# A graph network on one core: query projection and its nonlinearity computed in the first gather instead of the second

## The chip, the core and the metric

The kernel runs on one core of a Trainium2 chip. The metric is device time in microseconds (us) of one execution. The core has a matrix engine (TensorE, PE in the profile), VectorE (DVE), ScalarE (ACT), GpSimd (POOL), SyncE (SP), which here only issues DMAs, and 16 DMA engines that all queues share. Each engine runs its own instructions in order and waits on semaphores for the others.

## The reference

One layer over 12500 nodes of width 256 and 212500 edges, all in float32. With xn = layernorm(x):

```
gnn:  agg = segment_sum((xn @ W)[src] * weight, dst) + b ; elu, twice (the second reads the first's output)
mix:  Q = elu(xn @ Wq) + 1 ; K = elu(xn @ Wk) + 1 ; v = (xn @ Wv) / L
      KV = sum over nodes of K^T v, per head ; Z = 1 / (Q . sum K + 1e-6)
      msg = layernorm(((Q @ KV) * Z * L) @ Wm) * g1 + b1
      h = relu(concat(xn, msg) @ W1) @ W2 ; mix = xn + layernorm(h) * g2 + b2
x = x + gnn + mix ; x = x + mixture_of_experts(layernorm(x))
```

Q is needed against KV, and KV is a sum over all nodes. Q itself depends on xn and Wq alone.

## The kernel before, in words

`program` runs five stages in turn: `prepare` (layernorm of x, tables, constants), `gather` for layer 1, `gather` for layer 2, `route` and `experts`.

A gather has 104 turns (`loops` of two, u = 0, 1, buffers by u). In each, GpSimd issues 16 indirect DMAs (line 460), each of which fetches 128 rows of 256 floats by the indices in `idx`; the rows are double-buffered by turn. GpSimd may start a turn when TensorE has begun the turn before, which releases the other half of `rows` (`rows_used`). TensorE multiplies the rows with one-hot selections (`sel`, line 411) in four groups of 32 matmuls (`window_products`, line 403), the first two groups when the first eight DMAs have landed, the others when all have. VectorE adds the four sums into `agg` at places that it loads from a table into registers (lines 494 to 500), and releases the next turn with `turn_added`.

Beside that, each gather carries dense work on tiles of 128 nodes, one tile a turn for the first 98 turns, cut into places between the groups: `mix.pe(pe, i, u, place)` is called ahead of the first group (place 0), behind the first, second and third (1, 2, 3) and behind the fourth (4), and `mix.dve` and `mix.act` have places of their own. The order on each engine is that of the calls.

In the first gather the mixer is `keys_values`: TensorE turns the tile (line 784), ScalarE copies it out as `xt`, TensorE projects keys and values (line 790) and adds their product to `kv_total` (796). `dense_first` follows eight turns behind: the layer's product `z`, its elu and the store of h.

In the second gather the mixer is `attend`. For tile t, `queries` times `m.kv` (961), VectorE's `message` (1037 to 1042), transposes (968), the product with w_m (974), layernorm, transposes (979), the hidden product (987, of `xt` and the normed message), relu, the output product (947), a second layernorm one turn later and the store of `mix` (926). For tile t + 1, in the same turn, it makes the queries: the tile is turned (933) behind the transposes of the message; ScalarE copies `xt` (1079); the product with w_q (940) stands behind the transposes of the normed message; VectorE takes min(q, 0) (1020) behind its adds and after the release of TensorE; ScalarE takes exp (1083) ahead of its relu; VectorE adds max(q, 0) (1055) at the head of the next turn. `dense_second` follows eight turns behind with the second layer's product, residual, layernorm and gate.

SyncE's turn issues the next idx (430) once the rows of two turns ago have landed, the next tile (917), the store of `mix` and waits for its landing (926 to 928), and then the dense stores and loads (1269 to 1277).

Of the kernel before, what the change touches and what calls it, by code (L numbers as in the profile page):

```python
# [12 lines left out]
P = 128  # L13
# [104 lines left out]
def prepare(nc, m):  # L118

    with ExitStack() as ctx:  # L120
        def sb(name, shape, dt):
# [54 lines left out]
            (m.w_q[:, :, :], m.in_w_q.rearrange("(k p) n -> p k n", p=P)),  # L176
# [173 lines left out]
def gather(nc, m, layer, source, mixer, denser):  # L350
# [4 lines left out]
    with ExitStack() as ctx:  # L355
# [63 lines left out]
        with nc.Block(f"gather{layer}") as block:  # L419
            @block.sync  # L420
            def _(sp):
                for u in range(2):
                    sp.dma_start(idx[:, u, :], m.in_src[u]).then_inc(idx_loaded[u], 16)
                    mix.load(sp, u, u)
                mix.load_weights(sp)
                dense.load_weights(sp)

                def turn(i, u):
                    sp.wait_ge(rows_loaded[u][BANKS - 1], 16 * GROUP * SUB * i)
                    sp.dma_start(idx[:, u, :], m.in_src[bass.ds(2 * i + u, 1)].rearrange("o p c -> (o p) c")  # L430
                                 ).then_inc(idx_loaded[u], 16)
# [300 lines left out]
def keys_values(nc, m, sb, sem, ps, shared):  # L732
# [3 lines left out]
    w_v = sb("w_v", [P, KD, D])  # L736
    tile = sb("kv_tile", [P, 2, D])
    xt = sb("kv_xt", [P, KD, P])
# [6 lines left out]
    total = ps("kv_total", KD, KVS)  # L745

    weights_loaded = sem("kv_weights_loaded")
# [16 lines left out]
    def load_weights(sp):  # L764
        for to, of in ((w_k, m.in_w_k), (w_v, m.in_w_v)):
            sp.dma_start(to[:, :, :], of.rearrange("(k p) n -> p k n", p=P)).then_inc(weights_loaded, 16)
# [4 lines left out]
    def pe_begin(pe):  # L771
        pe.wait_ge(weights_loaded, 32)

        nc.tensor.matmul(total[:, :, :], m.ident[:, :], m.zeros[:, :].rearrange("p (k n) -> p k n", k=KD),
                         start=True, stop=False)

    def pe(pe, i, u, place):
        t = 2 * i + u
        if not has_tile(i, u):
            return  # L780
        if place == 0:
            pe.wait_ge(tile_loaded[u], 16 * i + 16)
            for h in range(KD):
                last = nc.tensor.transpose(turned[:, h, :], tile[:, u, h * P:(h + 1) * P], m.ident[:, :])
            last.then_inc(tile_turned, 1)
        if place == 1:
            pe.wait_ge(xt_ready, t + 1)
            for n, w in enumerate((w_k, w_v)):
                for k in range(KD):
                    last = nc.tensor.matmul(proj[n][:, 0, :], xt[:, k, :], w[:, k, :], start=(k == 0), stop=(k == KD - 1))  # L790
# [23 lines left out]

    def act(act, i, u, place):
        t = 2 * i + u
        if place or not has_tile(i, u):
            return
        act.wait_ge(tile_turned, t + 1)
        nc.scalar.copy(xt[:, :, :], turned[:, :, :]).then_inc(xt_ready, 1)  # L820
# [6 lines left out]
        nc.scalar.activation(k_exp[:, :], k_min[:, :], ACT.Exp).then_inc(k_exp_ready, 1)  # L827

# [15 lines left out]
    mix.dve, mix.act, mix.after = dve, act, after  # L844
    mix.store = lambda sp, i, u: None
# [5 lines left out]
def attend(nc, m, sb, sem, ps, shared):  # L851
# [6 lines left out]
    q_min = sb("q_min", [P, KD, P])  # L858
    queries = q_min
# [17 lines left out]
    tile_ps = ps("tile_ps", KD, P)  # L877
    query_ps = tile_ps
# [7 lines left out]
    tile_turned = sem("tile_turned")  # L886
    xt_ready = sem("xt_ready")
    query_projected = sem("query_projected")
    q_min_ready = sem("q_min_ready")
    q_exp_ready = sem("q_exp_ready")  # L890
    queries_ready = sem("queries_ready")
# [38 lines left out]
    def turn_tile(pe, t, u, i):  # L930
        pe.wait_ge(tile_loaded[u], 16 * i + 16)
        for h in range(KD):
            last = nc.tensor.transpose(tile_ps[:, h, :], tile[:, u, h * P:(h + 1) * P], m.ident[:, :])
        last.then_inc(tile_turned, 1)

    def project_queries(pe, t, u):
        pe.wait_ge(xt_ready, t + 1)
        for h in range(KD):
            for k in range(KD):
                last = nc.tensor.matmul(query_ps[:, h, :], m.w_q[:, k, h * P:(h + 1) * P], xt[:, u, k, :],  # L940
                                        start=(k == 0), stop=(k == KD - 1))
        last.then_inc(query_projected, 1)

# [7 lines left out]
    def pe_begin(pe):  # L951
        turn_tile(pe, 0, 0, 0)
        project_queries(pe, 0, 0)

    def pe(pe, i, u, place):
        t = 2 * i + u
        if place == 1:
            if has_tile(i, u):
                pe.wait_ge(queries_ready, t + 1)
                for h in range(KD):  # L960
                    last = nc.tensor.matmul(num_ps[:, h, :], queries[:, h, :], m.kv[:, h, :], start=True, stop=True)
# [3 lines left out]
        if place == 2 and has_tile(i, u):  # L965
# [4 lines left out]
            if has_tile(i, u, 1):  # L970
                turn_tile(pe, t + 1, 1 - u, i + u)
# [4 lines left out]
        if place == 4 and has_tile(i, u):  # L976
# [4 lines left out]
            if has_tile(i, u, 1):  # L981
                project_queries(pe, t + 1, 1 - u)
# [35 lines left out]
    def min_query(dve, t):  # L1018
        dve.wait_ge(query_projected, t + 1)
        nc.vector.tensor_scalar(q_min[:, :, :], query_ps[:, :, :], 0.0, None, ALU.min).then_inc(q_min_ready, 1)  # L1020

# [25 lines left out]
    def dve_begin(dve):  # L1047
        min_query(dve, 0)

    def dve(dve, i, u, place):  # L1050
        t = 2 * i + u
        if place == 0 and has_tile(i, u):
            dve.wait_ge(q_exp_ready, t + 1)

            nc.vector.scalar_tensor_tensor(queries[:, :, :], query_ps[:, :, :], 0.0, q_min[:, :, :],
                                           ALU.max, ALU.add).then_inc(queries_ready, 1)
# [5 lines left out]
        if place == 2:  # L1062
            if not before_first(i, u, 1) and has_tile(i, u, -1):
                output(dve, t - 1, 1 - u)
            if has_tile(i, u):
# [11 lines left out]
    def copy_tile(act, t, u):  # L1077
        act.wait_ge(tile_turned, t + 1)
        nc.scalar.copy(xt[:, u, :, :], tile_ps[:, :, :]).then_inc(xt_ready, 1)

    def exp_query(act, t):
        act.wait_ge(q_min_ready, t + 1)
        nc.scalar.activation(q_min[:, :, :], q_min[:, :, :], ACT.Exp).then_inc(q_exp_ready, 1)

    def act_begin(act):
# [3 lines left out]
        copy_tile(act, 0, 0)  # L1089
        exp_query(act, 0)  # L1090

    def act(act, i, u, place):
        t = 2 * i + u
        if place == 0:
# [5 lines left out]
            if has_tile(i, u, 1):  # L1100
                copy_tile(act, t + 1, 1 - u)
        if place == 1 and has_tile(i, u):
            guess_sd(act, t, 0)
        if place == 2 and has_tile(i, u):
# [5 lines left out]
            if has_tile(i, u, 1):  # L1110
                exp_query(act, t + 1)
# [3 lines left out]
    mix.load, mix.free, mix.store = load, free, store  # L1115
    mix.pe_begin, mix.pe, mix.dve_begin, mix.dve, mix.act_begin, mix.act = pe_begin, pe, dve_begin, dve, act_begin, act
    mix.pe_end = mix.dve_end = mix.act_end = lambda engine: None
# [785 lines left out]
def program(nc, ins, out, scratch):  # L1903
# [8 lines left out]
    m.mix = scratch("mix", [NP, D], F32)  # L1912
    m.x2 = scratch("x2", [UNITS * P, D], F32)
# [4 lines left out]
    with ExitStack() as ctx:  # L1918
# [20 lines left out]
        m.w_q = sb("w_q", [P, KD, D])  # L1939
# [72 lines left out]
```

## Time and profile before

| | us |
|---|---|
| median of 3 runs | 5139.43 |
| lowest, highest | 5133.67, 5143.25 |
| profiled execution | 5136.3 |
| its span | 5134.5 |
| mean granted clock of TensorE | 0.847 of full |
| busy: PE, DVE, ACT, POOL | 4113.3, 2643.0, 846.1, 3474.6 |
| moved by DMA | 639.48 MB, mean 125 GB/s |

The span runs from the first to the last instruction, 1.8 us less than the execution's time. Busy times overlap, so they don't add up to the span. The first gather lies at about 150 to 2265 us, the second at 2275 to 4441, routing and experts behind it. `[2.42 <-DMA rows<-h,idx]` behind an instruction means that its engine had idled 2.42 us before it and that this DMA ended the wait. A granted clock of 1 is 2.4 GHz, 0.5 is 1.2 GHz.

### The profile page before, as it was taken

What the parts mean: (1) busy time and instruction counts of PE and PEld (TensorE: products, weight loads), DVE (VectorE), ACT (ScalarE), POOL (GpSimd) and SP (SyncE); (2) the same over time, 40 slices, a digit from 0 to 9 for tenths busy, and PEclk for the clock granted to TensorE, in tenths of its full rate; (3) what the DMA queues carried; (4) which work ended last, traced back from release to release, by engine and by line L of the source; (5) the groups of instructions that cost most, each with busy time, mean ns of one, the idle gap of its engine ahead of it and who ended that gap; (6) DMA issues with size and microseconds to landing.
All of it is one profiled execution on the core that took longest, in us unless ns stands there. A gap on an engine that the chain in (4) does not pass through costs nothing. (4 is left out here: it accounts for less than half of the span.)

```text
span 5134.5 us, 87736 instructions
## 1 busy us (share of the span) xinstructions
PE 4113.3 (80%) x24996; PEld 3765.1 (73%) x24997; DVE 2643.0 (51%) x9389; ACT 846.1 (16%) x2617; POOL 3474.6 (68%) x3768
## 2 busy tenths in 40 slices
PE   0477777777777777759989898899888998689998
PEld 0476776767766667658888888888888887568887
DVE  7433333333333333345676666666666765554444
ACT  2001000010000000001222222222222221241111
POOL 0577777777777777757777777777777777235554
PEclk9867777777777777658999999999999998599999
DMA  7444444444444444434455545555555455322222
GB/s 212 134 116 119 117 118 118 119 118 118 118 119 118 118 118 119 115 84 118 138 148 148 152 145 146 145 153 146 146 150 150 144 146 152 99 68 76 73 73 69
DMA packets 361208, 639.48 MB, mean 125 GB/s; under 512 B 105581, under 2 KB 230381, under 8 KB 360989
## 3 DMA queue, kind: packets, MB, share of 16 engines
q0 software_dynamic: 171840, 469.16, 32.2%
q1 hardware_dynamic: 181621, 155.12, 9.9%
q10 hardware_dynamic: 7632, 13.77, 0.7%
q8 instruction: 61, 1.00, 0.1%
q14 instruction: 54, 0.44, 0.0%
HBM read 548.73 MB, written 89.00 MB: 124 GB/s over the span
## 5 line engine op out<-in xcount | busy, mean ns | idle before, releaser
L403 PEld LDWEIGHTS sums<-sel,rows 128*128 128x128 f32 x13312 | 1939.0, 227 | 782.7 <-DMA rows<-xn,idx 414.2
L403 PE MATMUL sums<-sel,rows 128*128 128x64 f32 x13312 | 1944.8, 310 | 688.9 <-DMA rows<-xn,idx 312.1
L460 POOL DMA_INDIRECT rows<-xn,idx x1664 | 1577.9, 948 | 644.8 <-issue 634.1
L460 POOL DMA_INDIRECT rows<-h,idx x1664 | 1585.7, 953 | 578.8 <-issue 527.1
L411 DVE TENSOR_SCALAR sel<-cols,rel_now,wgt_now 128x64 f32<-128x64 f32 x3360 | 781.8, 338 | 7.8
L417 DVE TENSOR_TENSOR agg<-agg,sums 128x128 f32 x832 | 240.6, 289 | 786.0 <-issue 570.0
L612 DVE TENSOR_TENSOR pre<-z,b_g 128x256 f32<-128x256 f32 x98 | 41.6, 425 | 558.2 <-PE z L607 558.2
L1816 PE MATMUL e_hidden_ps<-tokens_t,w 128*128 128x256 f32 x1248 | 277.9, 381 | 0.9 <-ACT tokens_t L1840 0.9
L1828 PE MATMUL y_ps<-w,e_hidden 128*128 128x256 f32 x1248 | 277.0, 380 | 0.0
L987 PE MATMUL hidden_ps<-xt,w 128*128 128x128 f32 x1568 | 250.1, 282 | 21.2 <-ACT msg_t L1108 21.0
L1816 PEld LDWEIGHTS e_hidden_ps<-tokens_t,w 128*128 128x128 f32 x1248 | 238.5, 191 | 34.1 <-ACT tokens_t L1840 1.3
L1828 PEld LDWEIGHTS y_ps<-w,e_hidden 128*128 128x128 f32 x1248 | 235.0, 191 | 30.5
L987 PE MATMUL hidden_ps<-msg_t,w 128*128 128x128 f32 x1568 | 239.4, 275 | 0.0
L987 PEld LDWEIGHTS hidden_ps<-xt,w 128*128 128x128 f32 x1568 | 208.3, 193 | 38.6 <-ACT msg_t L1108 38.6
L947 PE MATMUL row_ps<-w,hidden 128*128 128x256 f32 x784 | 215.9, 426 | 0.0
L987 PEld LDWEIGHTS hidden_ps<-msg_t,w 128*128 128x128 f32 x1568 | 207.1, 192 | 0.0
L790 PE MATMUL kv_proj<-w_k,kv_xt 128*128 128x256 f32 x392 | 198.0, 661 | 0.0
L808 DVE TENSOR_SCALAR k_min<-kv_proj 128x256 f32<-128x256 f32 x98 | 41.6, 425 | 282.1 <-PE kv_proj L790 282.1
L947 PEld LDWEIGHTS row_ps<-w,hidden 128*128 128x128 f32 x784 | 164.8, 221 | 23.3
L974 PE MATMUL row_ps<-w_m,msg_t 128*128 128x256 f32 x392 | 114.4, 416 | 65.0 <-ACT msg_t L1099 65.0
L790 PE MATMUL kv_proj<-w_v,kv_xt 128*128 128x256 f32 x392 | 164.7, 567 | 0.0
L1014 ACT ACTIVATE ln_var<-var 128x1 f32<-128x1 f32 x196 | 39.7, 203 | 729.1 <-DVE var L996 729.1
(227 smaller groups left out, 4701.9 us busy)
## 6 DMA issues: line engine op xcount, KB each, us to landing
rows<-xn,idx POOLq DMA_INDIRECT x1664
rows<-h,idx POOLq DMA_INDIRECT x1664
w<-in_ffn_w SPq DMA_DIRECT2D x16, 1024.0 KB, 7.8
ln_rows<-in_x SPq DMA_DIRECT2D x52, 256.0 KB
xn<-ln_normed ACTq DMA_DIRECT2D x52, 256.0 KB, 4.4
kv_tile<-xn SPq DMA_DIRECT2D x98, 128.0 KB, 2.2
h<-h_rows SPq DMA_DIRECT2D x98, 128.0 KB, 2.1
tile<-xn SPq DMA_DIRECT2D x98, 128.0 KB
```

The costliest lines, as they stand in the source:

```text
L403: last = nc.tensor.matmul(sums[:, g, h, :], rows[:, u, k, h * P:(h + 1) * P], sel[:, u, k, :], start=(c == 0), stop=(c == GROUP - 1))
L411: last = nc.vector.tensor_scalar(sel[:, u, k, :], m.cols[:, :], rel_now[:, u, k:k + 1], wgt_now[:, u, k:k + 1], ALU.is_equal, ALU.mult)
L417: return nc.vector.tensor_tensor(window, window, sums[:, g, :, :], ALU.add)
L460: nc.gpsimd.indirect_dma_start(out=rows[:, u, k, :], out_offset=None, in_=source, in_offset=bass.IndirectOffsetOnAxis(ap=idx[:, u, k:k + 1 ...
L612: nc.vector.tensor_tensor(pre[:, :], z, b_g1[:, :], ALU.add).then_inc(pre_ready, 1)
L790: last = nc.tensor.matmul(proj[n][:, 0, :], xt[:, k, :], w[:, k, :], start=(k == 0), stop=(k == KD - 1))
L808: nc.vector.tensor_scalar(k_min[:, :], proj[0][:, 0, :], 0.0, None, ALU.min).then_inc(k_min_ready, 1)
L947: last = nc.tensor.matmul(row_ps[1], hidden[:, o, :], m.w_2[:, o, :], start=(o == 0), stop=(o == F1 // P - 1))
L974: last = nc.tensor.matmul(row_ps[0], msg_t[:, k, :], m.w_m[:, k, :], start=(k == 0), stop=(k == KD - 1))
L987: last = nc.tensor.matmul(hidden_ps[:, o, :], m.w_1[:, k, o * P:(o + 1) * P], of, start=(k == 0), stop=(k == 2 * KD - 1))
L1816: last = nc.tensor.matmul(hidden_ps[f % HB], m.w1[u][:, k, f * P:(f + 1) * P], tokens_t[:, k, :], start=(k == 0), stop=(k == KD - 1))
L1828: last = nc.tensor.matmul(y_ps[tt], hidden[:, f, tt * P:(tt + 1) * P], m.w2[u][:, f, :], start=(f == 0), stop=(f == FC - 1))
```

## The change

The first gather computes the queries and stores them, and it stores the transposed rows `xt` as well; the second loads both. w_q is loaded with w_k and w_v and no longer among the constants of `prepare`. In `keys_values` `xt` gets two buffers and there are new buffers for `q_min` and `queries` and a bank for the product. SyncE calls `mix.load_more` behind `mix.store`, and `mix.stored` at the end.

In `gather`:

```diff
                     mix.load(sp, u, u)
+                    mix.load_more(sp, 0, u)
...
                     if has_tile(i - 1, u):
                         mix.store(sp, i - 1, u)
+                    if has_tile(i, u):
+                        mix.load_more(sp, i, u)
                     dense.sp(sp, i - 1, u)
...
+                mix.stored(sp)
                 dense.sp_end(sp)
```

In `keys_values`, the first gather (`exp_query` is called behind `exponential` of the dense part, as ScalarE's place 2):

```diff
+        if place == 2:          # TensorE
+            if not before_first(i, u, 1):
+                wait_apart(pe, queries_ready, t, m.pe_passed)
+            for h in range(KD):
+                for k in range(KD):
+                    last = nc.tensor.matmul(query_ps[:, h, :], w_q[:, k, h * P:(h + 1) * P], xt[:, u, k, :],
+                                            start=(k == 0), stop=(k == KD - 1))
+            last.then_inc(query_projected, 1)
...
                                            ALU.max, ALU.add).then_inc(keys_ready, 1)   # VectorE, place 2
+            dve.wait_ge(query_projected, t + 1)
+            nc.vector.tensor_scalar(q_min[:, :, :], query_ps[:, :, :], 0.0, None, ALU.min).then_inc(q_min_ready, 1)
+        if place == 3:
+            if not before_first(i, u, 2):
+                wait_apart(dve, q_stored[u], 32 * i, m.passed)
+            dve.wait_ge(q_exp_ready, t + 1)
+            nc.vector.scalar_tensor_tensor(queries[:, u, :, :], query_ps[:, :, :], 0.0, q_min[:, :, :],
+                                           ALU.max, ALU.add).then_inc(queries_ready, 1)
...
+        if not before_first(i, u, 2):     # ScalarE, ahead of the copy of xt
+            wait_apart(act, q_stored[u], 32 * i, m.act_passed)
...
+    def exp_query(act, i, u, place):
+        if place == 2 and has_tile(i, u):
+            act.wait_ge(q_min_ready, 2 * i + (u + 1))
+            nc.scalar.activation(q_min[:, :, :], q_min[:, :, :], ACT.Exp).then_inc(q_exp_ready, 1)
...
+    def store(sp, i, u):
+        t = 2 * i + u
+        sp.wait_ge(xt_ready, t + 1)
+        sp.dma_start(m.xt[bass.ds(t * P, P), :], xt[:, u, :, :].rearrange("p k n -> p (k n)")).then_inc(q_stored[u], 16)
+        sp.wait_ge(queries_ready, t + 1)
+        sp.dma_start(m.qt[bass.ds(t * P, P), :], queries[:, u, :, :].rearrange("p k n -> p (k n)")
+                     ).then_inc(q_stored[u], 16)
```

In `attend`, the second gather:

```diff
     def load(sp, t, u):
         sp.dma_start(tile[:, u, :], m.xn[bass.ds(t * P, P), :]).then_inc(tile_loaded[u], 16)
+        sp.dma_start(queries[:, u, :, :], m.qt[bass.ds(t * P, P), :].rearrange("p (k n) -> p k n", k=KD)
+                     ).then_inc(queries_loaded[u], 16)
+    def load_more(sp, i, u):
+        if not before_first(i, u, 2):
+            sp.wait_ge(hidden_done, 2 * i + (u - 1))
+        t = 2 * i + u
+        sp.dma_start(xt[:, u, :, :], m.xt[bass.ds(t * P, P), :].rearrange("p (k n) -> p k n", k=KD)
+                     ).then_inc(xt_loaded[u], 16)
     def free(sp, i, u):
+        sp.wait_ge(num_ready, 2 * i + (u + 1))
         sp.wait_ge(base_ready, 2 * i + (u + 1))
...
         if place == 1:          # TensorE
-                pe.wait_ge(queries_ready, t + 1)
+                wait_apart(pe, queries_loaded[u], 16 * i + 16, m.pe_passed)
...
-            if has_tile(i, u, 1):
-                turn_tile(pe, t + 1, 1 - u, i + u)
             pe.wait_ge(msg_t_ready, t + 1)
...
-            if has_tile(i, u, 1):
-                project_queries(pe, t + 1, 1 - u)
+            wait_apart(pe, xt_loaded[u], 16 * i + 16, m.pe_passed)
             pe.wait_ge(norm_t_ready, 2 * t + 2)
...
-        if place == 0 and has_tile(i, u):       # VectorE
-            dve.wait_ge(q_exp_ready, t + 1)
-            nc.vector.scalar_tensor_tensor(queries[:, :, :], query_ps[:, :, :], 0.0, q_min[:, :, :],
-                                           ALU.max, ALU.add).then_inc(queries_ready, 1)
...
+                wait_apart(dve, tile_loaded[u], 16 * i + 16, m.passed)
                 nc.vector.tensor_tensor(result[:, u, :], tile[:, u, :], m.ln2_b[:, :], ALU.add).then_inc(base_ready, 1)
...
-        if place == 3 and has_tile(i, u, 1):
-            min_query(dve, t + 1)
...
-            if has_tile(i, u, 1):               # ScalarE
-                copy_tile(act, t + 1, 1 - u)
...
-            if has_tile(i, u, 1):
-                exp_query(act, t + 1)
             act.wait_ge(hidden_done, t + 1)
```

The calls that made tile 0's queries ahead of the second gather's loop (`pe_begin`, `dve_begin`, two in `act_begin`) go too.

## Rows read from the trace of the kernel before

**Rows 1.** The page, 40 slices: POOL busy, TensorE's granted clock, in tenths.

```profile
POOL 0577777777777777757777777777777777235554
PEclk9867777777777777658999999999999998599999
```

**Rows 2.** Line 460: ns min, median, max; first and last start.

```profile
L460 POOL DMA_INDIRECT rows<-xn,idx x1664: 942/946/1094, 151.1 to 2243.8; - x185
L460 POOL DMA_INDIRECT rows<-h,idx x1664: 940/946/1698, 2275.8 to 4407.9; - x185
```

**Rows 3.** Waits of POOL, 300 to 2100 us: us in total, times, longest us.

```profile
POOL rows L460 <- issue: 428.3, 1406, 0.3
```

**Rows 4.** Waits of POOL, 2275 to 4409 us.

```profile
POOL rows L460 <- issue: 527.1, 1608, 10.0
POOL rows L460 <- DMA idx<-in_src: 41.2, 34, 31.1
POOL rows L460 <- PE sums L403: 10.6, 22, 3.5
```

**Rows 5.** Timeline of POOL: start, us, instruction, [idle before <-releaser].

```profile
3039.84 0.94 POOL L460 DMA_INDIRECT rows<-h,idx  x1 [1.88 <-issue]
```

**Rows 6.** Timeline of VectorE, from one turn's adds to the next turn's.

```profile
3053.58 1.56 DVE L417 TENSOR_TENSOR agg<-agg,sums 128x128 f32 x4 [3.11 <-issue]
3055.68 0.42 DVE L1020 TENSOR_SCALAR q_min<-tile_ps 128x256 f32<-128x256 f32 x1 [0.53 <-DVE agg L417]
3056.58 0.42 DVE L1055 SCALAR_TENSOR_TENSOR q_min<-tile_ps,q_min 128x256 f32<-128x256 f32 x1 [0.48 <-ACT q_min L1083]
...
3074.11 1.56 DVE L417 TENSOR_TENSOR agg<-agg,sums 128x128 f32 x4 [3.58 <-issue]
```

**Rows 7.** Timeline of TensorE, the same turn and the one before.

```profile
3043.49 0.38 PE L933 MATMUL tile_ps<-ident,tile 128*128 128x128 f32 x2
3044.12 1.13 PE L974 MATMUL row_ps<-w_m,msg_t 128*128 128x256 f32 x4 [0.24 <-ACT msg_t L1099]
...
3050.31 1.06 PE L940 MATMUL tile_ps<-xt,w_q 128*128 128x128 f32 x8
...
3055.80 1.97 PE L403 MATMUL sums<-sel,rows 128*128 128x64 f32 x16 [0.59 <-DVEq L517]
```

**Rows 8.** Waits of TensorE, 2500 to 4250 us.

```profile
PE sums L403 <- DVEq L517: 100.6, 81, 2.3
```

**Rows 9.** Timelines of SyncE and POOL; the page's DMA issues (us to landing).

```profile
3011.64 0.33 SPq L430 DMA_DIRECT2D idx<-in_src  x1
...
3016.45 0.95 POOL L460 DMA_INDIRECT rows<-h,idx  x1 [0.30 <-issue]
...
h<-h_rows SPq DMA_DIRECT2D x98, 128.0 KB, 2.1
```

**Rows 10.** Timelines of TensorE and POOL in the first gather.

```profile
1514.58 3.68 PE L403 MATMUL sums<-sel,rows 128*128 128x64 f32 x16 [4.74 <-DMA rows<-xn,idx]
...
1535.96 3.67 PE L403 MATMUL sums<-sel,rows 128*128 128x64 f32 x16 [4.43 <-DVEq L517]
...
1541.79 0.95 POOL L460 DMA_INDIRECT rows<-xn,idx  x1 [0.30 <-issue]
```

**Rows 11.** The page, DMA queues: packets, MB, share of 16 engines.

```profile
q1 hardware_dynamic: 181621, 155.12, 9.9%
```

**Rows 12.** Windows: busy (count) of PE, PEld, DVE, ACT, POOL; clock, DMA share.

```profile
2334.00:2480.00 146.00, 133.14 (x957) 126.19 (x958) 83.94 (x310) 25.11 (x79) 110.67 (x117) 0.91 0.43 123
...
3000.00:3500.00 500.00, 449.79 (x3325) 420.20 (x3324) 345.33 (x1295) 112.95 (x393) 372.82 (x391) 0.96 0.51 147
```

**Rows 13.** Timeline of TensorE in the second gather's first turns.

```profile
2370.65 5.77 PE L403 MATMUL sums<-sel,rows 128*128 128x64 f32 x32 [2.42 <-DMA rows<-h,idx]
...
2376.64 1.91 PE L940 MATMUL tile_ps<-xt,w_q 128*128 128x128 f32 x8
```

**Rows 14.** Waits of POOL, 2335 to 2780 us.

```profile
POOL rows L460 <- issue: 105.7, 347, 0.3
```

More of the change, by code:

```diff
@@ L175, in prepare @@
         consts = [
-            (m.w_q[:, :, :], m.in_w_q.rearrange("(k p) n -> p k n", p=P)),
             (m.w_m[:, :, :], m.in_w_m.rearrange("(k p) n -> p k n", p=P)),
@@ L736, in keys_values @@
     w_v = sb("w_v", [P, KD, D])
+    w_q = sb("w_q", [P, KD, D])
     tile = sb("kv_tile", [P, 2, D])
-    xt = sb("kv_xt", [P, KD, P])
+    xt = sb("kv_xt", [P, 2, KD, P])
+    q_min = sb("q_min", [P, KD, P])
+    queries = sb("queries", [P, 2, KD, P])
     k_min = sb("k_min", [P, D])
@@ L745, in keys_values @@
     total = ps("kv_total", KD, KVS)
+    query_ps = ps("query_ps", KD, P)
+    query_projected = sem("query_projected")
+    q_min_ready = sem("q_min_ready")
+    q_exp_ready = sem("q_exp_ready")
+    queries_ready = sem("queries_ready")
+    q_stored = [sem(f"q_stored{u}_") for u in range(2)]
     weights_loaded = sem("kv_weights_loaded")
@@ L764, in load_weights @@
     def load_weights(sp):
-        for to, of in ((w_k, m.in_w_k), (w_v, m.in_w_v)):
+        for to, of in ((w_k, m.in_w_k), (w_v, m.in_w_v), (w_q, m.in_w_q)):
             sp.dma_start(to[:, :, :], of.rearrange("(k p) n -> p k n", p=P)).then_inc(weights_loaded, 16)
@@ L771, in pe_begin @@
     def pe_begin(pe):
-        pe.wait_ge(weights_loaded, 32)
+        pe.wait_ge(weights_loaded, 48)
         nc.tensor.matmul(total[:, :, :], m.ident[:, :], m.zeros[:, :].rearrange("p (k n) -> p k n", k=KD),
@@ L789, in pe @@
                 for k in range(KD):
-                    last = nc.tensor.matmul(proj[n][:, 0, :], xt[:, k, :], w[:, k, :], start=(k == 0), stop=(k == KD - 1))
+                    last = nc.tensor.matmul(proj[n][:, 0, :], xt[:, u, k, :], w[:, k, :], start=(k == 0), stop=(k == KD - 1))
             last.then_inc(projected, 1)
+        if place == 2:
[6 more added lines that the diff above has]
+            last.then_inc(query_projected, 1)
         if place == 3:
@@ L818, in act @@
             return
+        if not before_first(i, u, 2):
+            wait_apart(act, q_stored[u], 32 * i, m.act_passed)
         act.wait_ge(tile_turned, t + 1)
-        nc.scalar.copy(xt[:, :, :], turned[:, :, :]).then_inc(xt_ready, 1)
+        nc.scalar.copy(xt[:, u, :, :], turned[:, :, :]).then_inc(xt_ready, 1)
         act.wait_ge(projected, t + 1)
@@ L827, in act, with act_both, stored @@
         nc.scalar.activation(k_exp[:, :], k_min[:, :], ACT.Exp).then_inc(k_exp_ready, 1)
+    def exp_query(act, i, u, place):
+        if place == 2 and has_tile(i, u):
+            act.wait_ge(q_min_ready, 2 * i + (u + 1))
+            nc.scalar.activation(q_min[:, :, :], q_min[:, :, :], ACT.Exp).then_inc(q_exp_ready, 1)
+    def act_both(engine, i, u, place):
+        act(engine, i, u, place)
+        exp_query(engine, i, u, place)
+    def store(sp, i, u):
[5 more added lines that the diff above has]
+                     ).then_inc(q_stored[u], 16)
+    def stored(sp):
+        for u in range(2):
+            sp.wait_ge(q_stored[u], 32 * (UNITS // 2))
     def after():
@@ L843, in keys_values @@
     mix.load, mix.free, mix.pe_begin, mix.pe, mix.pe_end = load, free, pe_begin, pe, pe_end
-    mix.dve, mix.act, mix.after = dve, act, after
-    mix.store = lambda sp, i, u: None
+    mix.dve, mix.act, mix.after = dve, act_both, after
+    mix.store, mix.stored = store, stored
+    mix.load_more = lambda sp, i, u: None
     mix.load_weights = load_weights
@@ L857, in attend @@
     xt = sb("xt", [P, 2, KD, P])
-    q_min = sb("q_min", [P, KD, P])
-    queries = q_min
+    queries = sb("queries", [P, 2, KD, P])
     den = sb("den", [P, KD, HC])
@@ L875, in attend @@
     inv_sd = sb("inv_sd", [P, 2, 1])
-    tile_ps = ps("tile_ps", KD, P)
-    query_ps = tile_ps
     num_ps, m.logit_ps = shared("num_ps", (KD, KVW), (1, NE))
@@ L885, in attend @@
     tile_loaded = [sem(f"tile_loaded{u}_") for u in range(2)]
[L886 to L891, printed above, removed]
+    xt_loaded = [sem(f"xt_loaded{u}_") for u in range(2)]
+    queries_loaded = [sem(f"queries_loaded{u}_") for u in range(2)]
     num_ready = sem("num_ready")
@@ L928, in store @@
         sp.sem_inc(result_free[u], 1)
[L930 to L942, printed above, removed]
     def mlp_output(pe, t):
@@ L949, in mlp_output @@
         last.then_inc(mlp_done, 1)
-    def pe_begin(pe):
-        turn_tile(pe, 0, 0, 0)
-        project_queries(pe, 0, 0)
     def pe(pe, i, u, place):
@@ L958, in pe @@
             if has_tile(i, u):
-                pe.wait_ge(queries_ready, t + 1)
+                wait_apart(pe, queries_loaded[u], 16 * i + 16, m.pe_passed)
                 for h in range(KD):
-                    last = nc.tensor.matmul(num_ps[:, h, :], queries[:, h, :], m.kv[:, h, :], start=True, stop=True)
+                    last = nc.tensor.matmul(num_ps[:, h, :], queries[:, u, h, :], m.kv[:, h, :], start=True, stop=True)
                 last.then_inc(num_ready, 1)
@@ L1016, in guess_sd @@
         nc.scalar.activation(guess[:, n, :], ln_var[:, n, :], ACT.Exp, scale=-0.5).then_inc(guess_ready[n], 1)
-    def min_query(dve, t):
-        dve.wait_ge(query_projected, t + 1)
-        nc.vector.tensor_scalar(q_min[:, :, :], query_ps[:, :, :], 0.0, None, ALU.min).then_inc(q_min_ready, 1)
     def output_variance(dve, t):
@@ L1045, in message @@
                                 .to_broadcast([P, KD, HC, HD]), ALU.mult).then_inc(msg_ready, 1)
-    def dve_begin(dve):
-        min_query(dve, 0)
     def dve(dve, i, u, place):
         t = 2 * i + u
-        if place == 0 and has_tile(i, u):
-            dve.wait_ge(q_exp_ready, t + 1)
-            nc.vector.scalar_tensor_tensor(queries[:, :, :], query_ps[:, :, :], 0.0, q_min[:, :, :],
-                                           ALU.max, ALU.add).then_inc(queries_ready, 1)
         if place == 1:
@@ L1073, in dve @@
                 normalise(dve, msg[:, :], 0).then_inc(normed_ready, 1)
-        if place == 3 and has_tile(i, u, 1):
-            min_query(dve, t + 1)
[L1077 to L1083, printed above, removed]
     def act_begin(act):
@@ L1088, in act_begin @@
             act.sem_inc(result_free[u], 1)
-        copy_tile(act, 0, 0)
-        exp_query(act, 0)
     def act(act, i, u, place):
@@ L1109, in act @@
                                      bias=m.ln1_b[:, h:h + 1]).then_inc(norm_t_ready, 1)
-            if has_tile(i, u, 1):
-                exp_query(act, t + 1)
             act.wait_ge(hidden_done, t + 1)
             nc.scalar.activation(hidden[:, :, :], hidden_ps[:, :, :], ACT.Relu).then_inc(hidden_ready, 1)
-    mix.load, mix.free, mix.store = load, free, store
-    mix.pe_begin, mix.pe, mix.dve_begin, mix.dve, mix.act_begin, mix.act = pe_begin, pe, dve_begin, dve, act_begin, act
-    mix.pe_end = mix.dve_end = mix.act_end = lambda engine: None
+    mix.load, mix.load_more, mix.free, mix.store = load, load_more, free, store
+    mix.pe, mix.dve, mix.act_begin, mix.act = pe, dve, act_begin, act
+    mix.stored = mix.pe_begin = mix.dve_begin = mix.pe_end = mix.dve_end = mix.act_end = lambda engine: None
     mix.load_weights = lambda sp: None
@@ L1912, in program @@
     m.mix = scratch("mix", [NP, D], F32)
+    m.xt = scratch("xt_rows", [UNITS * P, D], F32)
+    m.qt = scratch("queries_rows", [UNITS * P, D], F32)
     m.x2 = scratch("x2", [UNITS * P, D], F32)
@@ L1938, in program @@
         m.valid = sb("valid", [P, NT])
-        m.w_q = sb("w_q", [P, KD, D])
         m.w_m = sb("w_m", [P, KD, D])
```

## The prediction

> **What bounds the kernel now.** I read the 40 slices first [rows 1]. Between the preparation and the expert stage lie two long flat stretches, the two gathers. POOL is at 7 tenths in both; TensorE's clock is at 0.7 in the first and at 0.9 in the second. An engine whose digit never moves may be the pace-maker, so the second view is POOL's instructions [rows 2]: 1664 indirect DMAs a gather, 151.1 to 2243.8 us and 2275.8 to 4407.9 us, that is 2092.7 and 2132.1 us, or 20.1 and 20.5 us for each of 104 turns of 16. The third is its waits [rows 3]: in the steady part of the first gather 428.3 us over 1406 issues, 0.305 each and never more. With the median issue of 0.946 us a turn can't be shorter than 16 x 1.25 = 20.0 us. The first gather is issue-bound, all of it.
>
> The second isn't quite. There POOL idles 527.1 + 41.2 + 10.6 = 578.9 us [rows 4]. 1664 x 0.305 = 507.5 of it is the fixed part, 31.1 lies before its first issue, 9.7 (10.0 less 0.3) is the pause until TensorE's first turn. The rest, 30.6 us, are waits near the edges of turns, for the half of `rows` that TensorE hasn't released; a typical one, behind a turn's first issue, is 1.88 us long [rows 5]. The first gather has none, so they aren't POOL's own.
>
> Who is late? VectorE, by its timeline over one turn [rows 6]: from adds to adds 3053.58 to 3074.11, 20.5 us. It waits 0.53 us ahead of q_min (the branch behind the adds), 0.48 us for ScalarE's exp, and 3.11 to 3.58 us of issue ahead of the adds (six values loaded into registers); nearly all the rest follows back to back. It is a serial loop of VectorE's own. TensorE waits for its release, 0.59 us ahead of that turn [rows 7], 100.6 us in 81 of 85 turns, 1.2 a turn [rows 8]. So the three paths are: VectorE 20.5 us a turn, POOL 20.0, TensorE 20.5 - 1.2 = 19.3.
>
> **The change, part by part.** *Second gather, VectorE:* q_min 0.42, the 0.48 us wait for ScalarE and queries 0.42 leave the serial loop: 20.5 - 1.3 = 19.2 us. The 0.53 stays, it is the branch. Next to be late is POOL. Bounds: 19.4, if half of the 0.48 turns up elsewhere, and 18.7, if the 0.53 goes too; both below 20.0.
>
> *Second gather, TensorE:* the two transposes of the tile and the queries' product go, 0.38 and 1.06 us [rows 7]. They don't shorten the path by as much, for each covers a wait. The transposes lie over ScalarE's copy of msg_t, and TensorE waits 0.24 us behind them even so [rows 7]; the product lies over ScalarE's writing of norm_t. Bounds 0 and 1.4 us; I take 0.3, nearer to nothing, since both waits end with ScalarE. Path 19.0 us, 1.0 below POOL's. ScalarE loses a copy and an exp, and its relu, queued behind that exp, comes sooner; nobody waited for it.
>
> *What it gives:* of POOL's 30.6 us of waits I let 3 stand, most of them at the first turn, which runs at half clock and where the product covers a wait too. -27.6; bounds 0 and -30.6. Between its memset and the first selection VectorE no longer makes q_min of tile 0: -0.4.
>
> *Second gather, SyncE:* two more loads a turn. Queries go out with the tile, more than a turn before use; xt goes out behind the store of `mix` and its landing, and queued behind it are the stores of x2 and xf, the loads of x_in and mix_in, and the next idx. That idx goes out at 3011.64, and POOL's first issue with it starts at 3016.45 [rows 9]: less POOL's pause of 0.30 and 2.1 us for landing (the nearest row is a store of 128 KB) 2.4 us are to spare, and one more issue takes as long as that of idx, 0.33, or a little over. Cost 0; with that cover gone some 0.4 us a turn, 40 us. The new waits of TensorE for queries and xt and of VectorE for the tile find data that landed over 10 us before.
>
> *First gather:* TensorE gets the product, 1.06 us at full and 1.91 at half clock [rows 13], between its second and third group of sums. It waits 4.74 us for rows ahead of its first group [rows 10]. Where VectorE's adds come last instead, all moves by up to 2 us: z, pre, adds, and the next group from 1535.96 to 1538, while POOL needs that release only when its issues of the turn are out, at 1541.79 + 0.95 [rows 10]. VectorE makes q_min inside its wait for z, and queries behind its release of TensorE; ScalarE idles. SyncE gets two stores; the second waits for queries just before the h store, which waits for VectorE's next step anyway. The buffers that wait for these stores are needed two turns later. Cost 0; bounds 0 and, if the product came on top of a TensorE that had become the later one, 0.2 us a turn above POOL's 20.0, +20.
>
> *DMA engines:* 2 x 98 x 128 KB are 25.7 MB a gather. q1 moved 155.12 MB in 9.9% of the time [rows 11], so 25.7 MB are 84 us of all 16 engines, 4 points. POOL's mean issue is 110.67 / 117 = 0.946 us at a share of 0.43 and 372.82 / 391 = 0.953 at 0.51 [rows 12]: if the 8 points do it, half of that, 0.0035 x 1664 = 5.9 us a gather. The median doesn't move [rows 2], so I take +1 each, between 0 and +5.9. *Preparation:* w_q leaves the queue ahead of the edge weights, on whose landing that stage ends: one issue, -0.4, bounds 0 and -1. In the first gather it lands under the memset of the sums.
>
> Sum on the profiled execution of 5136.3 us (span 5134.5): -27.6 - 0.4 + 2 - 0.4 = -26.4, 5109.9. The median of the runs is 3.1 above it: **5113 us**.
>
> **TensorE's clock** is where the trace warns. In the first eight turns of the second gather there is no dense work, TensorE's path is shorter by more than it will be after the change, and POOL paces. There TensorE waits 2.42 us for rows, and then 32 matmuls take 5.77 us and the product 1.91 [rows 13], where 16 take 1.97 and the product 1.06 [rows 7]: 1.2 instead of 2.4 GHz, 3 to 4 us lost over the turn, call it 4. That stretch has 0.91 of the clock, the full turns 0.96 [rows 12]. With 1.0 us to spare a turn such a spell can be paid every fourth turn, and if it needs a wait for rows it won't come oftener: a TensorE that is behind has none. In between it may fall back by some 8 us (half a turn less a landing) before POOL waits. The stretch from 2335 to 2780 has these spells and no POOL wait above 0.3 us [rows 14].
>
> The Trainium skill, TensorE: Matmul & The Clock Gate, section "HAM oscillation — how this bites in real kernels", has a kernel that waits for data between bursts start every burst cold. By that rule a TensorE that now waits for rows would lose its clock in each turn, and rival B would be the forecast. The trace agrees for a wait of 2.42 us; that POOL isn't held up by it is the trace's, not the page's.
>
> **Rivals.** *A, the clock takes half.* With gaps where the removed work was, the full turns get the clock of the first eight: 19.0 x 0.96 / 0.91 = 20.0, level with POOL, and half of its waits stay, +12: 5125. Against: VectorE, not TensorE, is the serial one.
> *B, slower.* Large spells come whether or not TensorE is behind, set off by those gaps at msg_t and norm_t. It decides where 19.0 + 4s passes 20.5, over three spells in eight turns; at one in two a turn takes 21.0, +0.5 x 98 = +49 on 5139: 5188. Against: 0.24 us at msg_t and the wait for VectorE are there now, at 0.96.
> *C, POOL's gaps are its own.* Those of 1.88 us stay; the timeline of the gather has nine, 9 x 1.6 = 14 us: 5127. Against: none in the first gather or in [rows 14].
> *D, the moved work costs in the first gather* its bound of +20: 5133.
>
> **Chances.** Forecast 62% (its own range 5104 to 5122), A 14%, B 7%, C 8%, D 9%. 0.2% is 10 us, about what a measurement here can tell from no change. Faster by more: 61 + 9 + 5 + 1 = 76%; within: 15%; slower: 9%, B and the tail of D. Eight times in ten: 5103 to 5136.
>
> **What would show it.** POOL's indirect DMAs of the second gather take 2104 us from first to last instead of 2132, and those of the first stay within 5 of 2092.7. In the full turns TensorE waits for rows where it waited for VectorE, and VectorE waits for sums ahead of its adds. Wrong: gaps at POOL's edges as now, a granted clock under 0.93 in the full turns, or a first gather over 2100 us.

## The result, and the profile after

| | before | after |
|---|---|---|
| median of 4 runs, us | 5136.65 | 5335.78 |
| lowest, highest | 5133.67, 5143.25 | 5317.01, 5344.33 |
| profiled execution, span | 5136.3, 5134.5 | 5339.7, 5338.0 |
| mean granted clock | 0.847 | 0.824 |

The change makes the kernel slower: ratio 1.0381, 95% interval 1.0350 to 1.0412. Forecast were 5113 us and a range of 5103 to 5136. (Of the experiment e6 below two of four runs took 1.8 and 2.0% longer than its fastest, at a lower clock, so its figures are those of the other two.)

POOL's indirect DMAs of the changed kernel (columns as in [rows 2]) show where:

```profile
L463 POOL DMA_INDIRECT rows<-xn,idx x1664: 940/946/1191, 149.2 to 2245.5; - x185
L463 POOL DMA_INDIRECT rows<-h,idx x1664: 940/946/1436, 2277.7 to 4612.0; - x185
```

The first gather takes 2096.3 us (2092.7 before), the second 2334.3 (2132.1): the whole loss, +202. One issue is as long as it was; POOL waits. Its waits in the second gather, which answer to [rows 4]:

```profile
POOL rows L463 <- issue: 469.8, 1472, 9.7
POOL rows L463 <- PE sums L402: 199.8, 43, 9.7
POOL rows L463 <- DMA idx<-in_src: 67.4, 21, 31.2
```

10.6 us of waits for TensorE's release have become 199.8, in 43 turns: every second one. TensorE in turn (its waits, 2780 to 4350 us):

```profile
PE turn_ps L1007 <- DVE msg L1074: 67.4, 29, 3.7
```

The wait for the message, up to 3.7 us, is new: before it came to 1.8 us in all. So VectorE is late. Its timeline from the adds of an odd turn:

```profile
3099.55 1.56 DVE L416 TENSOR_TENSOR agg<-agg,sums 128x128 f32 x4 [3.46 <-issue]
3106.17 0.18 DVE L472 COPY rel_now<-dst_rel 128x16 f32 x1 [5.06 <-issue]
```

Between these two VectorE does no work and waits for no engine that the profile names, for 5.06 us; in [rows 6] the adds had 0.53 behind them. Over 2780 to 4350 us it is 186.5 us in 35 cases, 5.33 each, against 0.7 behind the adds of even turns, where only the `if` of the further windows stands. The odd turn is the second of a round: there the loop jumps back as well. (In the kernel before, that jump lies behind q_min, under the 0.48 us wait for ScalarE's exp.) The DMA queues of 3000 to 3500 us (packets, MB, share of 16 engines) have a row that the same stretch of the kernel before has not:

```profile
q14 instruction: 54, 0.44, 0.3%
```

In the whole execution that queue went from 54 packets to 261. It looks as if VectorE fetched its code again in every round; the experiments put that to the test. The last view is TensorE's clock in the full turns (columns as in [rows 12]), 0.96 before:

```profile
2780.00:3200.00 420.00, 353.29 (x2277) 327.68 (x2278) 240.13 (x919) 74.73 (x252) 275.79 (x290) 0.85 0.49 142
```

### The profile page after: what moved, and what is told of

It is laid out like the page before. It is cut to its first block and busy times, and to the rows that moved or that the text cites. A ratio compares the mean times of both kernels' runs of the same rounds, so it can differ in the third digit from the quotient of the medians.

```text
span 5338.0 us, 88695 instructions
## 1 busy us (share of the span) xinstructions
PE 4188.8 (78%) x24800; PEld 3824.8 (72%) x24801; DVE 2644.8 (50%) x9389; ACT 830.3 (16%) x2519; POOL 3482.6 (65%) x3768
## 5 line engine op out<-in xcount | busy, mean ns | idle before, releaser
L402 PEld LDWEIGHTS sums<-sel,rows 128*128 128x128 f32 x13312 | 1966.6, 230 | 777.5 <-DMA rows<-xn,idx 525.0
L402 PE MATMUL sums<-sel,rows 128*128 128x64 f32 x13312 | 1967.1, 312 | 680.2 <-DMA rows<-xn,idx 467.2
L1023 PE MATMUL hidden_ps<-xt,w 128*128 128x128 f32 x1568 | 282.9, 309 | 92.9 <-ACT msg_t L1118 92.9
L1023 PEld LDWEIGHTS hidden_ps<-xt,w 128*128 128x128 f32 x1568 | 238.7, 218 | 119.3 <-ACT msg_t L1118 119.3
L1023 PE MATMUL hidden_ps<-msg_t,w 128*128 128x128 f32 x1568 | 265.9, 297 | 0.0
L1023 PEld LDWEIGHTS hidden_ps<-msg_t,w 128*128 128x128 f32 x1568 | 234.0, 214 | 0.0
L1011 PE MATMUL row_ps<-w_m,msg_t 128*128 128x256 f32 x392 | 135.8, 478 | 67.9 <-ACT msg_t L1111 67.9
```

What stands on the lines that cost most here:

```text
L402: last = nc.tensor.matmul(sums[:, g, h, :], rows[:, u, k, h * P:(h + 1) * P], sel[:, u, k, :], start=(c == 0), stop=(c == GROUP - 1))
L1011: last = nc.tensor.matmul(row_ps[0], msg_t[:, k, :], m.w_m[:, k, :], start=(k == 0), stop=(k == KD - 1))
L1023: last = nc.tensor.matmul(hidden_ps[:, o, :], m.w_1[:, k, o * P:(o + 1) * P], of, start=(k == 0), stop=(k == 2 * KD - 1))
```

## The experiments

Theory F: the jump's target is no longer at hand and must be fetched, because of where VectorE's code lies. An instruction takes 64 bytes; in the compiled programs VectorE's loop of the second gather takes the places 3813 to 4136 before (324 instructions) and 3846 to 4166 after (321), counted without the labels. The rivals were TensorE's clock by itself (T), and the added loads and waits (S). To move the loop without touching it I issue instructions that only count up a semaphore nobody waits for. They run once, ahead of the loop:

```diff
                 take(0, 0)
                 dve.wait_ge(agg_zeroed, 1)
+                if layer == 2:
+                    for _ in range(100):      # e1; e3: 33, in the kernel before; e4: 50
+                        dve.sem_inc(m.passed, 1)
```

e2 has the 100 on ScalarE, behind `mix.act_begin(act)`. In e3 one of the 33 is merged with another instruction by the compiler: the loop moves by 32.

> The changed kernel, with 100 instructions added on VectorE that only count up a semaphore that nobody waits for, issued once, ahead of VectorE's loop of the second gather. The loop's work is untouched; its code lies 100 instructions further on. Theory F (fetch): in the changed kernel VectorE's loop code (321 instructions in the compiled program) has come to lie so that it touches three blocks of 256, and has to be fetched anew in every round of two turns; the 5.1 to 5.6 us of idle time ahead of rel_now in every second turn and the 54 instruction packets from 3000 to 3500 us are that. Moved on by 100 it lies in two blocks: packets to near 0, the idle time ahead of rel_now under 1 us in every turn, POOL's second gather from 2334 to 2100 to 2115 us, total 5105 to 5125. Theory T (TensorE): the slow turns come from TensorE's lower clock and the cover that the removed work gave; the place of VectorE's code does nothing and the total stays at 5335. Theory S (the added loads and waits): also 5335.

> Control: the changed kernel with the same 100 instructions on ScalarE instead of VectorE, at the same point. ScalarE's loop has 42 instructions and no stall. Theory F: VectorE's code lies as before, so nothing changes: 5335 within 8. A theory by which any disturbance of the start of the second gather would help expects the same as with the instructions on VectorE.

> The kernel before, with 33 such instructions on VectorE ahead of its loop of the second gather. That puts the loop (324 instructions) one instruction away from where the changed kernel has its own, and changes no work. Theory F: the loss appears without the change: 5.1 us more of idle time ahead of the first instruction of every second turn, instruction packets in the second gather as in the changed kernel, POOL's second gather at 2330 to 2370 us, total 5335 to 5375. Theories T and S: nothing, 5137 within 8.

> The changed kernel with 50 of them on VectorE. By theory F the total has two values and no others: the low one (5105 to 5125) or the high one (5335), according to which side of a block's edge the loop's last instruction falls; between 35 and 64 lies the step, so this one may go either way. A cost that grew with the distance moved would lie half way.

| | median, us | ratio to before, 95% | second gather, us | packets |
|---|---|---|---|---|
| e1 | 5118.31 | 0.9967 (0.9955 to 0.9978) | 2111.8 | 57 |
| e2 | 5369.18 | 1.0452 (1.0412 to 1.0492) | 2355.8 | 262 |
| e3 | 5259.84 | 1.0240 (1.0223 to 1.0258) | 2259.1 | 260 |
| e4 | 5473.00 | 1.0654 (1.0634 to 1.0673) | 2485.0 | 261 |

A hundred instructions that do nothing, on VectorE, take 217 us away; on ScalarE they don't. And 33 of them give the kernel before, with no change in it, the packets and the stall. T and S fall as first causes. Two sizes I had wrong. e2 came out 33 us above the changed kernel, which F doesn't explain and no run here does. And e3 lost 125 us, not 200 to 240. There the stall comes behind q_min:

```profile
3116.00 0.42 DVE L1058 SCALAR_TENSOR_TENSOR q_min<-tile_ps,q_min 128x256 f32<-128x256 f32 x1 [3.23 <-issue]
```

VectorE idles 3.2 us a round more around the adds and this jump than in the kernel before; the changed kernel idles 4.2 more than e1. And F's "two values and no others" failed: e4 is far above the changed kernel. Its timeline says why:

```profile
3134.47 0.72 DVE L416 TENSOR_TENSOR agg<-agg,sums 128x128 f32 x2 [3.51 <-issue]
3135.70 0.71 DVE L416 TENSOR_TENSOR agg<-agg,sums 128x128 f32 x2 [0.51 <-DVE agg L416]
3141.28 0.17 DVE L472 COPY rel_now<-dst_rel 128x16 f32 x1 [4.87 <-issue]
...
3141.61 0.31 DVE L410 TENSOR_SCALAR sel<-cols,rel_now,wgt_now 128x64 f32<-128x64 f32 x1
3143.37 1.87 DVE L410 TENSOR_SCALAR sel<-cols,rel_now,wgt_now 128x64 f32<-128x64 f32 x8 [1.45 <-issue]
```

VectorE stops a second time behind the first selection, and the adds are split two and two. The splits lie behind the 8th and the 264th instruction of the loop: 256 apart. So code comes in blocks of 256 instructions (16 KB), and from the compiled place 3896 of this loop the loaded code stands 192 places on: 3896 + 192 + 8 = 4096 = 16 x 256. With that, all loops have places:

| | loop, loaded | behind the edge at 4352 |
|---|---|---|
| before | 4005 to 4328 | 0: two blocks |
| after | 4038 to 4358 | 7: three |
| e3 | 4037 to 4360 | 9: three |
| e4 | 4088 to 4408 | 57: three, and 8 ahead of 4096 |
| e1 | 4138 to 4458 | 107, and the next edge is 4608: two |

As few as seven instructions behind the edge make the 217 us between e1 and the changed kernel. The Trainium skill, Runtime: NRT & Kernel Launch, section "Instruction fetch mechanics", has it so: an engine other than TensorE holds two blocks of 256 instructions, and a taken branch to a block that isn't there stops it until a DMA has brought it. The runs agree: two blocks, no such packets from 3000 to 3500 us; three, 4.9 packets of 8 KB a round ((261 - 54) / 42; the loop has 42 rounds, not the 46 of my expectations).

The next four put that to the test by a single instruction, and measure a stall without a fetch. The instructions now stand in the preparation, inside VectorE's wait for the edges:

```diff
                 nc.vector.memset(m.eps[:, :], LN_EPS).then_inc(eps_set, 1)
+                for _ in range(58):           # e6: 57
+                    dve.sem_inc(m.passed, 1)
                 dve.wait_ge(edges_loaded, 32)
...
                     t = 2 * i + u
+                    if layer == 2 and u == 0 and not isinstance(i, int):
+                        for _ in range(60):   # e7; e8: 30; not in e5 and e6
+                            dve.sem_inc(m.passed, 1)
                     dense.dve(dve, i, u, 0)
```

> The changed kernel with 58 counting instructions on VectorE, now in the preparation, inside its 8.79 us wait for the first edges, where they cost nothing (100 of them between the first two selections of the second gather took 7.0 us and stretched POOL's wait in the second turn from 3.5 to 9.3 us). From the run with 50: there the idle time split the 16 selections 1 to 15 and the four adds 2 to 2, the 8th and the 264th instruction of the loop's 321, so the edges of blocks of 256 lie behind these two, and the loaded code stands 192 places behind the compiled one. With 58 the loop starts exactly on an edge and ends 321 places on, in the second block. Theory F: fast, and 5.8 us faster than with the 100: 5112, between 5107 and 5118, POOL's second gather 2106 us. A theory by which 100 instructions helped by anything but the position (a later start of the second gather) expects 5335.

> The same with 57, one instruction fewer. The loop's first instruction is now the last of its block, and the loop touches three blocks, with 64 instructions in the third. Theory F: slow again, by as much as the run with 50 instructions ahead of the loop, which had 8 in the first block and 57 in the third: 5440 to 5500. Any theory without blocks of 256 expects the time of the run with 58.

> The run with 58, and at the head of each round of two turns of VectorE's loop in the second gather 60 counting instructions: a delay of 60 x 0.07 = 4.2 us per round without any fetching (the loop is 381 instructions long and still in two blocks), the size of the stall in the changed kernel (5.35 less 1.13 us that the jump takes anyway). It measures what such a stall is worth. If only VectorE's serial path counts: 2 x 19.2 + 4.2 = 42.6 us a round against POOL's 40.2, +2.4 x 46 rounds = +110, 5220. If what hangs on it (TensorE, which idles and gets 1.2 GHz for part of the next turn) pays as in the changed kernel, +222: 5335, with a granted clock of 0.83 to 0.87 from 2780 to 4000 us. If the fetches themselves disturb POOL or the DMA queues, the total stays well below 5335 here.

> The same with 30: 2.1 us per round. VectorE's path comes to 40.5 us a round, 0.3 above POOL's. If only the path counts: +0 to +15, 5112 to 5127. If any wait that TensorE gets costs it its clock: over +60.

| | median, us | ratio to before, 95% |
|---|---|---|
| e5, 58 | 5125.06 | 0.9969 (0.9957 to 0.9981) |
| e6, 57 | 5462.53 and 5494.33 | 1.062, 1.068 |
| e7, 58 and delay of 60 | 5459.32 | 1.0620 (1.0603 to 1.0636) |
| e8, 58 and delay of 30 | 5424.39 | 1.0545 (1.0529 to 1.0561) |

One instruction fewer costs 337 to 369 us, as expected from e4. e5 beats both kernels; it is 16 us faster than before. (All of this group ran on a chip where before took 5142.38, so ratios compare better than medians.) At the jump e6 has 7.2 us of idle time in the mean, and e5 has what is left of it:

```profile
3109.45 1.56 DVE L418 TENSOR_TENSOR agg<-agg,sums 128x128 f32 x4 [3.69 <-issue]
3112.16 0.18 DVE L474 COPY rel_now<-dst_rel 128x16 f32 x1 [1.15 <-issue]
```

e7 and e8 have 57 and 56 packets, so they don't fetch. Their delays came out longer than I had set them. VectorE's wait at that place in e8 (2780 to 4350 us):

```profile
DVE rel_now L474 <- issue: 129.7, 33, 3.9
```

That is 3.93 us each against 1.15 in e5: 2.8 us for the 30 instructions, not 2.1; in e7 it is 6.70, so 5.6 us for the 60, more than the stall of 4.2 that they were to copy. Even so they overturned my arithmetic of the path: 2.8 us a round should cost (2 x 19.2 + 2.8 - 40.2) x 42 = 42 us and cost 299, 7 a round; 5.6 should cost 160 and cost 334. TensorE's timeline of e8 behind such a delay, and in e5 at the same place:

```profile
3129.93 0.69 PE L1012 MATMUL turn_ps<-ident,msg 128*128 128x128 f32 x2 [2.03 <-DVE msg L1079]
3131.51 2.08 PE L1016 MATMUL row_ps<-w_m,msg_t 128*128 128x256 f32 x4 [0.89 <-ACT msg_t L1116]
...
3120.25 1.13 PE L1013 MATMUL row_ps<-w_m,msg_t 128*128 128x256 f32 x4 [0.46 <-ACT msg_t L1113]
```

In e5 the product with w_m takes 1.13 us, in e8 2.08: 1.2 instead of 2.4 GHz, once TensorE has waited 2.03 us for the message and 0.89 for its copy. (In the changed kernel the same product takes 2.08 us behind waits of 2.65 and 1.14.) The clock of the full turns is 0.78 to 0.80 in e8, 0.94 to 0.96 in e5. If that is the cause, more work in the wait must make the kernel faster:

```diff
         if place == 2 and has_tile(i, u):
+            if u == 0 and not isinstance(i, int):
+                for _ in range(12):           # e9, e10, e12; e11: 24
+                    nc.tensor.matmul(fill_ps[:, 0, :], m.w_m[:, 0, 0:P], m.w_m[:, 0, 0:P], start=True, stop=True)
             pe.wait_ge(msg_ready, t + 1)
```

> The run with the delay of 30 instructions, and on TensorE, in the even turns of the second gather's loop, 12 matmuls of 128 x 128 on constants into an unused bank, ahead of the wait for the message. In the run without them that wait is 2.0 us in every round, and the granted clock is 1.2 GHz from the next matmul on: the product with w_m takes 2.08 us instead of 1.13, the next 16 matmuls of the sums 3.52 instead of 1.90. The 12 take 12 x 0.133 = 1.6 us of those 2.0; they do no work that the output needs. Theory C (clock): the delay costs 299 us because the wait for the message costs TensorE its clock, so with the wait filled the clock stays near 0.95 and the total falls to 5125 to 5150, though there is more work. Theory P (path): the delay is paid on a path of waits, and the matmuls change nothing or add up to 1.6 us a round: 5424 to 5500.

> Control: the same 12 matmuls without the delay. TensorE's path of a round goes from 38.0 to 39.6 us, below POOL's 40.2. Both theories: 5125 within 8, or up to 10 above where a turn has no slack.

> The changed kernel with its stall as it is, and 24 such matmuls (3.2 us) at the same place, where TensorE waits up to 3.7 us for the message. It parts the 217 us that the position of VectorE's loop costs. Theory C: the stall of 4.2 us a round alone makes VectorE's path 42.6 us against POOL's 40.2, +110; the rest, some 107, is TensorE's clock and goes: 5220 to 5260, clock over 0.90, the instruction packets as many as before (54 in 3000 to 3500 us). Theory P: 5335 or more.

> The changed kernel with its stall, and 12 calls on TensorE ahead of the wait for the message in the even turns; the trace has two matmuls for each call in float32, 24 of 0.12 us, 2.9 us in all (and 5.8 for the 24 calls of the run before, after which VectorE waited 1.7 us a turn for TensorE). Theory C: clock over 0.93 in the full turns, what remains is the stall, 4.2 us a round less the 0 to 2.4 that POOL has over VectorE: 5210 to 5260, below the 5299 of the run with 24. Theory P: 5335 or more.

| | median, us | ratio to before, 95% | second gather, us |
|---|---|---|---|
| e9, e8 and fill | 5194.15 | 1.0112 (1.0096 to 1.0129) | 2187.2 |
| e10, e5 and fill | 5201.60 | 1.0132 (1.0115 to 1.0149) | 2195.7 |
| e11, after and 24 | 5298.85 | 1.0316 (1.0298 to 1.0333) | 2293.7 |
| e12, after and 12 | 5233.03 | 1.0187 (1.0170 to 1.0204) | 2225.0 |

e9: useless work makes the delayed kernel 230 us faster, though not down to 5150, for the fill isn't free. I had sized it wrong (2.9 us, not 1.6), and e10, my control, lost 85 us of the second gather, 2.0 a round. The granted clock of the full turns is back at 0.95 to 0.96, so at least 230 of the 299 us were the clock. e9 is no slower than e10 (-7), but that doesn't make it the whole: in e10 the fill itself is on the path (VectorE waits 42.4 us for the product with w_m behind it), and a delay of VectorE may hide beside it. e11's fill, 5.8 us, was too large: VectorE waited for the product with w_m behind it, 50.4 us in 30 turns. e12, with half, parts the changed kernel's loss. A window of e12:

```profile
2780.00:3200.00 420.00, 361.93 (x2669) 337.84 (x2668) 257.27 (x992) 80.20 (x268) 294.26 (x310) 0.96 0.53 153
```

The clock is back, the stall still there (189.2 us in 36 cases), and the second gather at 2225.0. Of 2334.3 - 2110.4 (e5) = 224 us, at least 109 were TensorE's clock. The other 115, 2.7 a round, are the stall on the path and whatever the fill costs; VectorE's arithmetic gives (2 x 19.2 + 4.2 - 40.2) x 42 = 101 for the stall. It doesn't reach POOL through TensorE alone: in 2780 to 4350 us POOL waits 86.6 us for idx, which SyncE sends late, and 29.7 for sums (e5: 2.7 and 2.4).

Two controls remain. e13 puts the 91 that align the loop into the preparation of the kernel before; e14 is e5 with `sp.sem_inc(queries_loaded[u], 16)` and the same for xt in place of the loads, from the third tile on.

> Control: the kernel before with 91 counting instructions on VectorE in the preparation, so that its loop of the second gather starts on the edge of a block, as in the changed kernel with 58. It lay in two blocks already. 5137 within 8; if lying on an edge were a gain of its own, it would be 10 or more faster.

> The changed kernel with 58, and the second gather's loads of queries and xt left out from the third tile on (SyncE counts up their semaphores instead), so later tiles get those of the first two. If the loads cost nothing but the 1 us forecast: the time of the run with 58 (0.9969 of before) within 0.001. If their traffic lengthens POOL's issues (mean 955 ns with them, 953 in the kernel before, x 1664) and the waits at idx: 4 to 12 us less, 0.994 to 0.996 of before.

e13: 5136.35, ratio 0.9999 (0.9989 to 1.0009). In the kernel before, an aligned loop is no gain of its own, so e5's gain is taken to be the change's. e14: 5115.62, 0.9956 (0.9939 to 0.9973), which overlaps e5's interval, and its profile has no shorter issue (956 ns in the mean, e5 955, e13 956) and no shorter second gather (2112.8): whether the loads cost a few us stays open.

## Why the prediction was wrong

**The step that failed** is VectorE's: "20.5 - 1.3 = 19.2 us. The 0.53 stays, it is the branch. Next to be late is POOL." The work left the loop as forecast, but in every second turn the 0.53 became 5.33 us. The 0.53 is the `if` behind the adds, and that stayed (0.7). The sum had no term for the loop's jump back, which lay behind q_min under the 0.48 us wait that the sum took out. What it costs depends on where its target lies, and the edit had moved the loop by 33 places: 0.4 us a round in two blocks (e5: 1.15 less 0.7), 4.6 in three. No bound of mine (18.7 to 19.4), no rival and no line of "what would show it" had the code's position in it. The trace of before couldn't show the danger. The compiled program showed half of it, a loop of 324 instructions, more than one block; that it ended 23 places short of an edge took the 192 as well, which only e4 gave. The stall on the path is at most 115 of the 224 us.

**The second step** is the clock: "if it needs a wait for rows it won't come oftener: a TensorE that is behind has none." The spells need no wait for rows. In the changed kernel they follow the wait for the message, as in e8. That is rival B's claim (spells come whether or not TensorE is behind) with another trigger, and it was worth at least 109 us, not its 49. Where the loop lies well it doesn't decide: e5 keeps 0.94 to 0.96, above the 0.93 named. At nearly the same place the kernel before loses 125 us (e3) at a clock of 0.90 to 0.92, the changed one 217 at 0.85. Part of that is the shorter stall (3.2 against 4.2 us a round); whether the moved work also covered TensorE's waits wasn't tried by itself.

**The other steps**, read from e5, against the profiled execution of before:

| | forecast | e5 |
|---|---|---|
| start of the first gather | -0.4 | -1.3 |
| first gather | +1 (0 to +20) | +2.7 (2095.4) |
| second gather, POOL's idle time | -27.6 | -25.0 (553.9) |
| second gather, POOL's busy time | +1 (0 to +5.9) | +3.5 (1589.2) |
| profiled execution | -26.4 | -20.4 (5115.9) |

```profile
L465 POOL DMA_INDIRECT rows<-h,idx x1664: 940/946/1696, 2277.7 to 4388.1; - x185
```

So the change is worth some -16 us (-10 to -23 by the intervals of e1 and e5) instead of -26, once its code lies well. POOL paces, and its gaps near the edges go: in e1 it has no issue gap above 0.3 us from 2780 to 4350 us (3.6 in the kernel before), which refutes rival C. D is refuted by the first gather. TensorE waiting for rows in the full turns came in e1 and not in e5, whose times agree. First e5, then e1:

```profile
PE sums L404 <- DVEq L522: 108.9, 73, 3.6
PE hidden_ps L1025 <- ACT msg_t L1120: 73.5, 75, 1.3
PE sums L404 <- DMA rows<-h,idx: 10.4, 8, 3.5
...
PE sums L402 <- DMA rows<-h,idx: 73.7, 67, 3.1
PE sums L402 <- DVEq L523: 39.7, 27, 3.2
```

Why the two differ in this no run shows. In e1 these waits cost no clock (0.95 to 0.96), so the prediction was right that a TensorE with such waits needn't be slower. The waits for ScalarE's copies have grown where the product lay over them (73.5 against 17.4 us for norm_t). VectorE's 0.53 a turn came to 0.9 (1.15 and 0.7 by turns), above my bound, yet below what POOL needs. The spare of TensorE was put at 1.0 us a turn; e10, where 2.0 of 2.9 us a round came through, gives an estimate of 0.45 at that place.

## What to carry to other kernels

Ahead of any edit of a kernel with a loop of more than 256 instructions on an engine, take from the compiled program where that loop begins and ends, and from a timeline what the loader adds: whether it spans two blocks or three cost some ten times what this edit is worth, and the edit itself moves it. When a kernel gets slower by the same idle time "issue" at each round's first instruction, look for instruction packets among the DMA queues before looking for a semaphore, and move the code by instructions that do nothing, once. A wait given to TensorE can cost more than its length: here 2.8 us of delay on VectorE, two of which TensorE waited for the message, cost seven.

## What the runs showed of the hardware

- VectorE's loaded code stood 192 places behind the compiled one. That the step lies between 57 and 58 was forecast from one timeline and held.
- The `if` behind the adds leaves 0.7 us of idle time on VectorE. With the jump back behind it, it is 1.15 us into code that is at hand and 5.33 into code that isn't.
- A counting instruction takes VectorE 0.09 us (30 of them 2.8, 60 of them 5.6). The 0.07 of my expectations came from 100 that lay partly under the selections ahead of them.
- Three blocks don't cost the same everywhere: with 7 instructions in the third, ratio 1.038; with 57 and 64, 1.065 and 1.062 to 1.068. The loss follows VectorE's added idle time at the edges: 3.2 us a round in e3, 4.2 in the changed kernel, 6.1 in e4, 6.4 in e6. The delays without a fetch don't fit that row: 2.8 us cost 299 us in e8, 5.6 cost 334 in e7.
